# A sixteen-layer float32 transformer kernel on one core: layer loops written out, and work moved between places of a layer

## The reference

```python
# L1, per batch element: S = 512 rows, D = 512, 16 heads of 32, feed-forward width 2048
x = _ln(src) * (1.0 + scale) + shift
q, k, v = x @ Wq + bq, x @ Wk + bk, x @ Wv + bv          # split into 16 heads
scores = einsum(q / sqrt(32), k) + attention_bias        # 512 x 512 for each head
probs = softmax(where(src_mask, -inf, scores))
x = x + (einsum(probs, v) @ Wo + bo)
h = _ln(x) * g2 + beta2
x = x + _gelu2(h @ W1 + b1) @ W2 + b2
# L2: y = ln(gelu(x @ down_W.T + down_b) through the chosen expert @ up_W.T + up_b + x) * gamma + beta
# L3: groups of four columns turned by theta and phi
```

## Time and profile before

| | |
|---|---|
| median of 3 runs (lowest to highest) | 5191.7 us (5175.97 to 5199.07) |
| profiled execution, own time | 5190.59 us |
| its span | 5188.7 us |
| granted TensorE clock, mean | 0.915 |
| PE busy | 4193.0 us, 81% |
| DVE busy | 3240.6 us, 62% |
| ACT busy | 2391.5 us, 46% |
| POOL busy | 2447.1 us, 47% |

### The profile page before, as it was taken

How to read it: one execution, slowest core, us unless ns; L and a number is a source line. 1 busy time by engine, 2 the same in 40 slices (tenths; PEclk the granted TensorE clock), 3 DMA queues, 4 the chain that set the end, 5 groups by cost and what they waited for, 6 DMA issues and landing times.

```text
span 5188.7 us, 80793 instructions
## 1 busy us (share of the span) xinstructions
PE 4193.0 (81%) x24872; PEld 3051.9 (59%) x24872; DVE 3240.6 (62%) x6332; ACT 2391.5 (46%) x4459; POOL 2447.1 (47%) x1164
## 2 busy tenths in 40 slices
PE   7985787888888787877878787878878787878788
PEld 3431565666666565656656565656656565656566
DVE  8972556565655656565665657575756656565656
ACT  0002544546364545545363645545363635445363
POOL 0000554545555554545555554545555554545455
PEclk9995899999999899999989899999999899999989
DMA  3223744535353634535363635535363636445362
GB/s 119 108 91 77 208 134 130 163 104 178 101 171 116 181 127 138 162 105 171 95 187 100 184 124 156 152 111 165 99 185 102 178 122 168 141 123 171 95 177 84
DMA packets 541110, 713.65 MB, mean 138 GB/s; under 512 B 45600, under 2 KB 257872, under 8 KB 540592
## 3 DMA queue, kind: packets, MB, share of 16 engines
q1 hardware_dynamic: 523728, 674.35, 44.2%
q10 hardware_dynamic: 16896, 33.56, 1.7%
HBM read 537.42 MB, written 35.72 MB: 110 GB/s over the span
## 4 chain that ended last, share of the span: by engine, by line
PE 32%; issue 18%; DVE 17%; SPq 10%; POOL 6%; ACT 3%; DMA 3%; DVEq 0%; ACTq 0%; POOLq 0%
PE bank L844 20%; SPq L534 10%; PE bank L889 4%; POOL prob L634 4%; PE bank L913 2%; DVE xin L1077 2%; PE bank L925 2%; DMA stack<-parts 2%; DVE prob L1115 2%; PE bank L853 1%; DVE wide L1203 1%; DMA prob<-in_fside_Bx16xSxS 1%; PE bank L948 1%; ACT gel L810 1%; ACT parts L814 1%
## 5 line engine op out<-in xcount | busy, mean ns | idle before, releaser
L634 POOL TENSOR_TENSOR prob<-prob,mask_add 128x1024 f32<-128x1024 f32 x520 | 1139.4, 2214 | 323.1 <-DMA prob<-in_fside_Bx16xSxS 322.6
L623 POOL TENSOR_TENSOR w<-w_raw,w 128x1024 fp32r<-128x1024 f32 x243 | 607.4, 2500 | 995.0 <-ACT w L693 993.5
L925 PE MATMUL bank<-ident,prob 128*128 128x128 f32 x4096 | 679.0, 292 | 122.3 <-ACT probT L720 102.6
L702 ACT ACTIVATE prob<-prob,low 128x512 f32<-128x512 f32 x1024 | 731.8, 716 | 99.0 <-DVE low L1115 96.5
L913 PE MATMUL bank<-stack 128*128 128x512 f32 x1024 | 505.6, 496 | 323.3 <-DVE low L1115 169.5
L1115 DVE CUSTOM_DVE_ANT_0 prob<-bank,prob 128x512 f32<-128x512 f32 x1024 | 699.4, 684 | 0.0
L925 PEld LDWEIGHTS bank<-ident,prob 128*128 128x128 f32 x4096 | 516.1, 149 | 291.7 <-ACT probT L720 82.3
L623 POOL TENSOR_TENSOR stack<-V,stack 128x1024 fp32r<-128x1024 f32 x145 | 348.5, 2405 | 639.0 <-ACT stack L693 638.6
L720 ACT ACTIVATE probT<-bank 128x512 f32<-128x512 f32 x768 | 451.5, 590 | 355.8 <-PE bank L925 354.6
L1114 DVE COPY fence<-cur 128x1 f32<-128x1 f32 x1024 | 154.0, 150 | 622.9 <-PE bank L913 597.0
L844 PE MATMUL bank<-xT,stack 128*128 128x512 f32 x1944 | 493.2, 404 | 46.8 <-DVE xT L1086 34.3
(11 more groups left out here) (180 smaller groups left out, 6599.7 us busy)
## 6 DMA issues: line engine op xcount, KB each, us to landing
prob<-in_fside_Bx16xSxS SPq DMA_DIRECT2D x520, 512.0 KB, 4.5
stack<-parts SPq DMA_DIRECT2D x1024, 128.0 KB, 2.4
V<-in_L_cond_W SPq DMA_DIRECT2D x256, 256.0 KB, 4.2
w_raw<-in_L_cond_W SPq DMA_DIRECT2D x256, 256.0 KB, 3.1
xin<-x SPq DMA_DIRECT2D x17, 1024.0 KB, 5.6
w_raw<-in_L_cond_Wv SPq DMA_DIRECT2D x68, 256.0 KB, 2.8
field<-in_x SPq DMA_DIRECT2D x16, 1024.0 KB, 5.3
x<-total ACTq DMA_DIRECT2D x16, 1024.0 KB, 5.8
```

The source lines that it names most:

```text
L623: pool.tensor_tensor(w[s][:, 1, :], w_raw[s], w[s][:, 0, :].bitcast(F32), ALU.subtract).then_inc(w_lo[s], 1)
L634: pool.tensor_tensor(half, half, mask_add[:, q:q + 1, :].to_broadcast([P, 2, S]), ALU.add).then_inc(bias_masked, 1)
L702: act.activation(prob[:, i, :], prob[:, i, :], ACT.Exp, bias=low[:, i:i + 1], scale=-1.0, accum_out=total[:, g % 2, i:i + 1]).then_inc(exp ...
L925: mm = t.transpose(turned[e % 2][:, k * P:(k + 1) * P], prob[:, i, k * P:(k + 1) * P], ident[:])
```

## The change

The layer loops and the feed-forward loops are written out in Python, with constant addresses and counts. Pass 16 prepares nothing for a layer 17. Within a layer:

- GpSimd adds `bo` to `xin` after the masks of group 3, not at the start of the layer; it adds `b2` to `res` after the split of chunk 4, not after that of chunk 2; after the four roots it waits until VectorE has made the low parts of `xT`.
- The split of the second half of Wo moves from the start of the layer to step 4 of group 3 on ScalarE, and behind the last masks on GpSimd.
- Two activations on one column (`warm`) are put where they make ScalarE load the tables for Exp and for the feed-forward's gelu earlier.
- `qk_wide` moves from steps 2 and 3 of a group to 0 and 1, with `q_hi`; `qk_lo_part` from 4 and 5 to 2 and 3; the split of the next query/key weights from step 4 to 2. The twelve pieces of a group's projection all lie in steps 5 to 15 of the group two before it (before: ten in steps 7 to 15, two in steps 0 and 1 of the next), and for group 1 in the seven lead blocks. SyncE issues the stack transfers ahead of bias transfer p = 2, before: ahead of p = 3.
- `adapt` follows chunks 8, 10, 12 and 14, before: 9, 11, 13 and 15. The roots for it follow chunks 6 to 9, before: 8 to 11.

```diff
@@ SyncE @@
                     for p in range(8):
-                        if p == 3:
+                        if p == 2:
                             sp.wait_ge(qk_hi, 2 * n + 4)
                             sp.wait_ge(qk_lo, 2 * n + 4)
@@ GpSimd @@
-                with pool.Fori(0, B) as b:
-
+                for b in range(0, B):
+
+                    more = b + 1 < B
+                    for g in range(G - 1):
+                        group(b, g)
+                    split_lo(1, ITEMS[1] * b + W1_O)
                     pool.wait_ge(turn_full, TURNS * b + KB)
                     pool.tensor_tensor(xin[:], xin[:], bcast(row["bo"]), ALU.add).then_inc(xin_biased, 1)
-                    split_lo(1, ITEMS[1] * b + W1_O)
-                    for g in range(G - 1):
-                        group(b, g)
                     for c in range(2):
                         split_lo(*chunk_item(b, 0, c))
                     for q in range(TB):
                         root(ROOTS * b + TB + q + 1, q)
-                    split_lo(*chunk_item(b, 0, 2))
-
+
+                    pool.wait_ge(turn_lo, TURNS * b + 2 * KB + START)
+                    for c in range(2, 4):
+                        split_lo(*chunk_item(b, 0, c))
+                    split_lo(*chunk_item(b, 1, 0))
                     pool.wait_ge(z2_ready, b + 1)
                     pool.tensor_tensor(res[:], res[:], bcast(row["b2"]), ALU.add).then_inc(res_biased, 1)
@@ ScalarE @@
-                        if i in (2, 3) and not last:
-                            q_hi(b, g + 1, i - 2, FILL_QK + g + 1)
-                        if i == 4 and not last:
+                        if i in (0, 1) and not last:
+                            q_hi(b, g + 1, i, FILL_QK + g + 1)
+                        if i == 4 and last:
+                            split_hi(1, ITEMS[1] * b + W1_O)
+                        if i == 2 and not last:
 
                             act.wait_ge(proj_full[1], FILLS * b + FILL_QK + g + 2 + START)
                             split_hi(0, ITEMS[0] * b + W0_QK + g + 2)
...
+                    act.activation(warm[:], minus_half[:, 0:1], ACT.Exp)
...
-                with act.Fori(0, B) as b:
-                    split_hi(1, ITEMS[1] * b + W1_O)
+                for b in range(0, B):
...
                     ctx_hi_part(b, G - 1)
+                    act.activation(warm[:], minus_half[:, 0:1], ACT.Gelu_apprx_sigmoid)
@@ TensorE @@
-                        if not last and i < 2:
-                            qk_piece(b, g + 1, 10 + i)
-                        if g + 2 < G and i >= 7:
-                            for p in range((i - 7) * 10 // 9, (i - 6) * 10 // 9):
+                        if g + 2 < G and i >= 5:
+                            for p in range((i - 5) * 12 // 11, (i - 4) * 12 // 11):
                                 qk_piece(b, g + 2, p)
...
-                    input_products(b + 1)
+                    if more:
+                        input_products(b + 1)
@@ VectorE @@
+                        if not last and i in (0, 1):
+                            qk_wide(b, g + 1, i, FILL_QK + g + 1)
                         if not last and i in (2, 3):
-                            qk_wide(b, g + 1, i - 2, FILL_QK + g + 1)
-                        if not last and i in (4, 5):
-                            qk_lo_part(b, g + 1, i - 4)
+                            qk_lo_part(b, g + 1, i - 2)
...
-                        if f >= 8 and f % 2:
+                        if f >= 8 and f % 2 == 0:
                             adapt(link, b + 1, (f - 8) // 2, ROOTS * b + 2 * TB)
...
-                    first_qk(b + 1)
-                    v.wait_ge(rstd_ready, ROOTS * (b + 1) + TB)
+                    if more:
+                        first_qk(b + 1)
+                    v.wait_ge(rstd_ready, final_root(b, TB - 1))
```

110 lines of the change are left out of this document (63 added, 47 removed).

## The result

| | kernel before | changed kernel |
|---|---|---|
| median of 5 runs | 5182.0 us (5171.9 to 5199.1) | 5045.7 us (5043.0 to 5074.6) |
| ratio to before, 95% interval | | 0.9746 (0.9716 to 0.9777) |
| profiled execution, its span | 5190.6, 5188.7 us | 5074.6, 5072.0 us |
| granted clock in it | 0.915 | 0.921 |
| instructions | 80793 | 69560 |

The change gains 2.5%, some 131 to 136 us, where 238 were forecast: 5045.7 lies just above the range of 4880 to 5040. The profiled execution of the changed kernel is the slowest of its five, 29 us above their median, so what it shows of single stages is up to 1.8 us a layer too long in sum.

The account below looks back on a forecast made before the run. No single engine was taken as the bound; time is lost where engines wait for each other. Five terms, 58 + 77 + 75 + 16 + 12 = 238 us, off the profiled 5190.6 gave 4953 us, range 4880 to 5040.

Parts of the forecast that it names:

- Term A: Start of a layer: the copy `cur` no longer waits for the `bo` addition, 3.9 us x 15 = 58 us (31 to 74).
- share of 0.5: Group transitions: 0.5 us taken off per layer for the earlier query/key weight split and the Wo split on ScalarE, together.
- reserve of 1.0: Start of a layer: 1.0 us allowed for the copy waiting on GpSimd's weight split, from a possible 0 to 2.8.
- Term B: Group transitions, three a layer: earlier stack transfers shorten TensorE's waits, 4.8 us x 16 = 77 us (0 to 151).
- the first rival: Transitions gain nothing: the stack wait is replaced by one for mask p = 2 or the split weight; 5030 us, chance 0.18.
- sign of being wrong: Wrong if a layer takes over 285 us, TensorE waits anew for split weights, or issue gaps appear without a branch.
- Term C: Second layer norm: `tok` 32 and `xT` 27 us without GpSimd's splits beside them, table load 16; 75 us (30 to 80).
- Term D: Feed-forward: tail 2.9 us gone, less 1.2 for a fourth `adapt` between chunks and 0.7 for `b2`; 16 us (-14 to 46).
- price put on the `b2` addition: Feed-forward: 0.7 us a layer for gelu subtractions made late by the addition; 1.5 if the exclusion rule is taken to its end.
- Term E: First layer and last pass: no normalisation wait or `adapt` stalls in the last, masks undelayed in the first; 12 us (5 to 20).
- The loops: Layer start: VectorE's branch issue gap of 1.0 us a pass goes, 14.5 us over 15 passes; other engines' branches gain nothing.
- The rival of starving engines: Straight-line code stalls an engine on instruction fetch, the gain all but eaten: 5167 us, no change; chance 0.03.

Follow-up runs that it names:

- e1: Changed kernel with the `bo` addition put back ahead of group 0, but behind VectorE's second score step: 4965.7 us, ratio 0.9564.
- e18: e1 with the splits of the last half of Wo back at the start of the layer, on ScalarE and GpSimd: 4939.5 us, ratio 0.9509.
- e2: e1 without its added wait, so the `bo` addition stands at the start of the layer as in the kernel before: 5024.2 us, ratio 0.9653.
- e4: Kernel before with all loops written out and no work for a 17th layer, nothing else moved: 5061.4 us, ratio 0.9754.
- e3: Changed kernel with the whole query/key schedule of before, stack transfers ahead of bias p = 3 included: 5076.0 us, ratio 0.9789.
- e17: e1 with the whole query/key schedule of before: 5003.9 us, ratio 0.9644.
- e8: e1 with a group's twelve query/key pieces only at steps 7 to 15, not from step 5: 4946.7 us, ratio 0.9504.
- e9: e1 with the stack transfers queued ahead of bias transfer p = 3, as in the kernel before: 4957.6 us, ratio 0.9532.
- e15: e10 with a one-column gelu added on ScalarE in each layer, ahead of the feed-forward's waits: 5134.6 us, ratio 0.9900.
- e10: Kernel before with only the feed-forward's two inner loops, on ScalarE and TensorE, written out: 5172.8 us, ratio 0.9967.
- e7: e1 with adaptations and roots back behind the odd widenings, as in the kernel before: 4946.8 us, ratio 0.9514.
- e12: e1 with the edits of e7, e8, e9 and e18 together: 4942.1 us, ratio 0.9535.

## Why the prediction was off

*The step that failed.* Term A took the `bo` addition away from the start of a layer, and the forecast gave its new place in group 3 no price: it said of the addition that it "blocks nothing that reads PSUM, as the score steps do". That is true of the score steps themselves and is not enough. The low part of the context reads SBUF, stands ahead of the last score step in the same queue, and was held for 4.49 us; TensorE then stood still for 4.00. The rule quoted there (SBUF — State Buffer, section "Who interferes with whom", of the Trainium skill) says that an instruction of VectorE with two SBUF inputs and one of GpSimd that reads SBUF shut each other out for their whole length; the row agrees, and it was applied to one of the two additions only. From the end of the stop on TensorE's granted clock was 0.50 for 6.80 us, which the forecast had not thought of either. Cost: 80 to 94 us by e1, 93 by the stage table (28.9 - 23.1 = 5.8 a layer). Of the remaining 1.1 a layer in that stretch 0.9 goes with the Wo split (e18), for which the forecast took off its share of 0.5. With the one term the forecast of 4953 would have been 5033 to 5047.

*Term A, start of a layer, 58.* Right. From the first of the output's last four operations to the end of the copy, VectorE takes 10.6 us before and 6.6 in the change: 4.0 us, 60 us in 15 layers, and e2 shows 46 to 58 for the addition. The first row of the table shows 5.2 - 2.1 = 3.1 of it, since the split mostly holds the copy now and mostly held the last operation ahead of it before. Two readings were off. In the change the split holds one of the two for some 2 us in every layer; it did so before in 9 of 15, and in the other 6 VectorE's branch gap of 2.4 us (14.5 in 6) lay over it. So the gap and the reserve of 1.0 were two sides of one thing. And with the loops written out and the addition still in its old place (e4) it is 8.2 us, so part of this term comes with the loops alone. The text also took the copy for a case of the rule that it quotes; that sentence is on two inputs in SBUF, and the copy has one. That it was held to the end of the addition is what the earlier trace rows show.

*Term B, transitions, 77.* Mis-sized: 22 (e3, by the ratios) to 41 (e17), between the forecast and the first rival. The wait for the stack fell by 96 us. But a wait for split weights of 117 us and one for masks of 84 took its place, and the text had named the first as a sign of being wrong. The 0.5 us taken off was far too little. The fall of one wait was booked as time, while waits of other engines rose; e8 and e9 show the same, 80 us off one wait worth 8 to 31. Which of the new waits sets the pace is open.

*Term C, second layer norm, 75.* 25.4 - 22.0 = 3.4 us a layer, 54 us of the 59 for `tok` and `xT`, at the durations forecast. The table load was worth more than the 16 us given to it: it stood in the feed-forward three times a layer, and e15 gives 35 to 38 us for the one that e10 leaves, with what it shifts.

*Term D, feed-forward, 16.* The tail fell by 2.9 us as forecast. The first half is 0.7 us longer than in e4 (42.8 to 42.1), which fits the price put on the `b2` addition and not the 1.5 that the rule taken to its end would give. The adaptations at even places cost 4.4 us a layer and not 1.2, so moving them loses 19 to 26 us by e7.

*Term E, the ends, 12.* Too small: the 17th layer's work alone costs 25 to 48.

*The loops.* They were given 1 us of issue gap a layer, with "nothing" for the other engines. They cost 79 to 84 us. Of these 59 are on ScalarE, most of it by table loads in the loop body (e15 gets 52 back with the loop over layers in place); the groups show them as x48, and the text followed the first. That the profile of before has 440.6 us of VectorE waiting for gelus, with a longest wait of 2.8 against 1.4 now, was there to be read. The rival of starving engines was rightly held small: in the whole span of the change VectorE shows 0.5 us of issue idle time and TensorE's matmuls 10.7, and ScalarE's 119.7 us ahead of the first split of a layer are gone.

So the sum came out nearly right for e1 (4966) by luck, through errors of both signs: loops and 17th layer too small by some 80, transitions and feed-forward too large by about as much. The change's own result is that less the one term left out.

## What to carry to other kernels

Before a GpSimd instruction is moved, list what stands in VectorE's queue during its whole length, not only what it meets first: here one operation with two SBUF inputs stopped the score step behind it, and TensorE with it. Look at the count and the idle time of ScalarE's table loads before pricing a loop: here a load inside a loop body sat behind the wait, and a dummy activation ahead of the wait took it off the path. And when an edit shortens a wait, look at what the other waits do; here 80 us off one of them were worth 8 to 31. After a stop of TensorE, look at the granted clock too.

## What was unexpected of the hardware

The copy `cur` of 128x8 takes 0.17 us (3 times) or 2.13 us (13 times) in the change and nothing between, and 4.30 us beside the `bo` addition (15 of 16 in e2). One layer of either kind, VectorE's last four operations of the output and the copy with GpSimd's split:

```profile
1952.64 4.31 DVE L1287 SCALAR_TENSOR_TENSOR res<-res,cur,tok 128x512 f32<-128x512 f32 x4
...
1955.35 3.81 POOL L627 TENSOR_TENSOR w<-w_raw,w 128x1024 fp32r<-128x1024 f32 x1 [15.17 <-ACT w L704]
...
1957.05 2.13 DVE L1195 COPY cur<-scal 128x8 f32<-128x8 f32 x1
```

```profile
1389.88 6.42 DVE L1287 SCALAR_TENSOR_TENSOR res<-res,cur,tok 128x512 f32<-128x512 f32 x4
...
1392.59 2.75 POOL L627 TENSOR_TENSOR w<-w_raw,w 128x1024 fp32r<-128x1024 f32 x1 [15.18 <-ACT w L704]
...
1396.41 0.17 DVE L1195 COPY cur<-scal 128x8 f32<-128x8 f32 x1
```

The rows read as taking turns. In the first layer the split arrives during the fourth operation, which ends at 1956.95 (1952.64 + 4.31); the split ends 2.2 us behind that, and the copy with it. In the second it arrives during the third; now the fourth operation is the one that is held, the four take 6.42 us in place of 4.31, and the copy is free. So the 2.13 us is what is left of the split when VectorE's last operation ends. The four operations and the copy together take 6.5 and 6.7 us in the two layers: what the copy doesn't lose, the operation ahead of it has lost.

Why the three small edits don't add up stays open. The mean granted clock doesn't follow the gains alone: it is 0.915 in the profiled executions of the kernel before and of e4, which is 128 us faster, 0.921 in the change, 0.931 in e1 and 0.940 in e12. In e1 it is the stretch behind the stop of TensorE that got its clock back; for e12 nothing was tried apart.
